# A new instruction order for a cross-attention kernel: fewer runs of small tiles on TensorE, fixed PSUM banks, four group slots

## The reference

```python
def layer0(x, c):
    q, k, v = heads(x @ Wq), heads(c @ Wk), heads(c @ Wv)        # 16 heads of 64
    logits = einsum('bhqd,bhkd->bhqk', q, k) / 8 + col_bias      # -20*(1-mask) on four columns
    out = einsum('bhqk,bhkd->bhqd', softmax(logits), v)
    return merge(out) @ Wo + bo + x

def layer(x, c):                                                 # layers 1, 2 and 3
    xn = x * rsqrt(mean(x * x) + 1e-5) * norm_w
    q, k, v = xn @ wq, c @ wk, c @ wv                            # 16 heads, 4 key-value heads, of 8
    attn = softmax(einsum('btgrd,bsgd->bgrts', q, k) / sqrt(8))
    return x + einsum('bgrts,bsgd->btgrd', attn, v) @ wo
```

## Time and profile before

| | |
|---|---|
| median of three runs | 1382.42 us (1378.57 to 1383.25) |
| span of the profiled execution | 1376.3 us |
| TensorE busy, matmuls | 1362.7 us, 99% of the span |
| TensorE busy, weight loads (overlap the matmuls) | 1055.6 us, 77% |
| VectorE, ScalarE, GpSimd busy | 1064.6, 1003.3 and 734.9 us: 77%, 73% and 53% |
| chain that ended last | TensorE 95%, ScalarE 2%, VectorE 2% |
| TensorE clock granted | 1.000 in all the span |

### The profile page before, as it was taken

The page is one execution under the profiler, slowest core; times in us unless marked ns, Lnnn a source line. Parts: engine busy times, 40 slices in busy tenths (PEclk is TensorE's granted clock), DMA queues, the critical chain, the costliest instruction groups (busy, mean ns, idle before and its releaser), DMA issues.

```text
span 1376.3 us, 59054 instructions
## 1 busy us (share of the span) xinstructions
PE 1362.7 (99%) x25494; PEld 1055.6 (77%) x25494; DVE 1064.6 (77%) x2258; ACT 1003.3 (73%) x2207; POOL 734.9 (53%) x851
## 2 busy tenths in 40 slices
PE   9999999999999999999999999999999999999997
PEld 7777777777777777777787777777777777777875
DVE  4487777987778977778777788777798777778776
ACT  4667777767778677777677786777776777767886
POOL 5355456654456545466554565544665445655553
PEclk9999999999999999999999999999999999999999
DMA  5010010000000010100001001001011010010000
GB/s 151 18 30 22 15 34 16 26 27 23 26 23 22 27 27 23 28 18 26 26 24 26 23 22 27 27 24 28 17 27 27 23 27 25 19 36 22 7 23 14
DMA packets 46003, 37.02 MB, mean 27 GB/s; under 512 B 17072, under 2 KB 41520, under 8 KB 45744
## 3 DMA queue, kind: packets, MB, share of 16 engines
q1 hardware_dynamic: 44576, 32.89, 8.8%
q10 hardware_dynamic: 1168, 0.36, 0.1%
HBM read 16.42 MB, written 4.19 MB: 15 GB/s over the span
## 4 chain that ended last, share of the span: by engine, by line
PE 95%; ACT 2%; DVE 2%; issue 0%; POOL 0%; DMA 0%; SPq 0%; POOLq 0%
PE psum L954 18%; PE psum L942 16%; PE psum L1009 10%; PE psum L1027 8%; PE psum L969 8%; PE psum L991 7%; PE psum L1055 7%; PE psum L1019 5%; PE psum L980 5%; PE psum L1063 4%; PE psum L1032 3%; PE psum L961 2%; PE psum L1038 2%; ACT E L1141 1%; ACT E L1136 1%; DVE st L1226 1%
## 5 line engine op out<-in xcount | busy, mean ns | idle before, releaser
L892 POOL TENSOR_TENSOR E<-E,st 128x512 f32<-128x512 f32 x488 | 497.3, 1044 | 168.1 <-DVE st L1238 159.4
L1136 ACT ACTIVATE E<-E,inv 128x512 f32<-128x512 f32 x384 | 273.4, 722 | 135.8 <-DVE E L1230 134.3
L1226 DVE TENSOR_REDUCE st<-psum 128x8 f32<-128x512 f32 x372 | 240.4, 673 | 145.5 <-PE psum L991 145.1
L1235 DVE TENSOR_REDUCE st<-E 128x8 f32<-128x512 f32 x488 | 321.2, 665 | 35.3 <-ACT E L1129 28.2
L1141 ACT COPY E<-psum 128x512 f32<-128x512 f32 x512 | 275.1, 609 | 33.7 <-PE psum L1009 33.5
L954 PE MATMUL psum<-wv,cT 128*128 128x374 f32 (+1 forms) x768 | 273.3, 486 | 0.3 <-issue 0.3
L1230 DVE TENSOR_TENSOR E<-psum,st 128x512 f32<-128x512 f32 x372 | 248.3, 677 | 0.3
L904 POOL TENSOR_TENSOR nt<-nt,powers 128x2 f32<-128x2 f32 (+1 forms) x102 | 19.9, 196 | 420.0 <-DVE nt L1265 400.2
L942 PE MATMUL psum<-cT,wk 128*128 128x256 f32 x1024 | 240.5, 383 | 0.2 <-DMA cT<-in_ctx_t 0.2
L942 PEld LDWEIGHTS psum<-cT,wk 128*128 128x128 f32 x1024 | 191.5, 190 | 34.8 <-issue 1.5
L954 PEld LDWEIGHTS psum<-wv,cT 128*128 128x128 f32 x768 | 138.2, 189 | 73.5 <-ACT V L1097 8.5
(11 more groups left out here) (68 smaller groups left out, 1632.2 us busy)
## 6 DMA issues: line engine op xcount, KB each, us to landing
KB<-K SPq DMA_DIRECT2D x1536, 8.0 KB
cT<-in_ctx_t SPq DMA_DIRECT2D x32, 256.0 KB, 2.8
xq<-in_x_t SPq DMA_DIRECT2D x32, 128.0 KB, 2.1
out<-xT SPq DMA_DIRECT2D x30, 128.0 KB, 1.8
wk<-in_L_xattn_Wk SPq DMA_DIRECT2D x3, 256.0 KB, 5.8
wv<-in_L_xattn_Wv SPq DMA_DIRECT2D x2, 374.0 KB, 8.6
wq<-in_L_xattn_Wq SPq DMA_DIRECT2D x1, 512.0 KB, 7.7
wo<-in_L_xattn_Wo SPq DMA_DIRECT2D x1, 512.0 KB, 4.4
```

Of the source, the lines that this page charges most:

```text
L892: e.tensor_tensor(E3, E3, wide(stat[s][u][:, 16:24]), ALU.mult).then_inc(g_nrm.sem, 1)
L1136: e.activation(E[s][u][:, :], E[s][u][:, :], ACT.Exp, scale=inv[s][:, u // 2:u // 2 + 1]).then_inc(a_exp.sem, 1)
L1226: e.tensor_reduce(stat[s][u][:, 0:8].rearrange("p (r h) -> p r h", r=2), scores_of[g, l, u], AX, ALU.max).then_inc(d_max.sem, 1)
L1235: e.tensor_reduce(stat[s][u][:, 8:16], heads(E[s][u][:, :]), AX, ALU.add).then_inc(d_sum.sem, 1)
```

## The change

The tables of all five engines are replaced, with ends for groups 0 to 6 and 26 to 31. TensorE's steps of one small-tile shape now stand next to each other more often. The number of slots `NS` goes from three to four, and steps of four different groups are in progress at once. The bank of each step comes from a table too (`PE_BANKS`, `BANK_ENDS`) in place of the rule. The transposes `t` of a layer become two steps of 16 records, one for each half, with their own waits and places. `x2` is done as 64-row transposes (two for each half, each into its own bank), in the same 64x128 tiles as `t`; ScalarE's square (L1157) reads the two banks in one instruction. A hook for aligning the program before chosen steps is there, but its list `FRESH` is empty, so nothing is emitted.

```diff
-NS = 3
+NS = 4
-PERIOD = 42.042923
+PERIOD = 41.111607
 PE_TIME = {
-    "pv": {1: (-307.00785,), 2: (-275.6979,), 3: (-251.97787,)},
+    "pv": {1: (87.69763,), 2: (127.91302,), 3: (168.09796,)},
...
+PE_BANKS = {
+    "k": {0: ("6", "7", "0", "6")},
...
+FRESH = set()
...
-        for kind, layers in {**table, **{k: {**table.get(k, {}), **v} for k, v in at_ends.get(g, {}).items()}}.items():
+        for kind, layers in at_ends.get(g, table).items():
...
             if kind == "t":
-                return [[("et", g, l, 2 * p + i)] for p in halves(g, u) for i in range(2)]
+                return [[("et", g, l, 2 * u + i)] for i in range(2)]
...
-            evictors = held_until(st)
-            if st[0] == "s" and l > 0:
-                at = min(([i, i + 1, j, j + 1] for i in range(5) for j in range(i + 2, 7)),
-                         key=lambda four: max(free[i] for i in four))
-            else:
-                at = sorted(sorted(range(8), key=lambda i: free[i])[:len(evictors)])
+            evictors, at = held_until(st), banks_of(*st)
...
-                if kind != "t":
-                    emptied(w, [ev for evs in before[st] for ev in evs])
+                emptied(w, [ev for evs in before[st] for ev in evs])
+                if (kind, l, u) in FRESH:
+                    e.addr_align(256, max_nops=0)
...
                 elif kind == "t":
                     w.wait_ge(l_ident, "ident")
-                    for n, p in enumerate(halves(g, u)):
-                        emptied(w, before[st][2 * n] + before[st][2 * n + 1])
-                        if late(g, l):
-                            w.wait_ge(a_exp, ("exp", g, l, 2 * p), ("exp", g, l, 2 * p + 1))
-                        else:
-                            w.wait_ge(g_nrm, ("nrm", g, l, 2 * p), ("nrm", g, l, 2 * p + 1))
...
+                    if late(g, l):
+                        w.wait_ge(a_exp, ("exp", g, l, 2 * u), ("exp", g, l, 2 * u + 1))
+                    else:
+                        w.wait_ge(g_nrm, ("nrm", g, l, 2 * u), ("nrm", g, l, 2 * u + 1))
...
                     for p in halves(g, u):
-                        m = e.transpose(bank[:, 128 * p:128 * p + 128], xT[s][:, 128 * p:128 * p + 128], ident[:, :])
+                        for i in range(2):
+                            rows = slice(64 * i, 64 * i + 64)
+                            m = e.transpose(psum[:, at[i], 64 * p:64 * p + 64], xT[s][rows, 128 * p:128 * p + 128],
+                                            ident[rows, rows])
...
-                        e.activation(QT[s][:, 2, tokens], bank[:, tokens], ACT.Square).then_inc(a_ev.sem, 1)
+                        e.activation(sq, x, ACT.Square).then_inc(a_ev.sem, 1)
```

More of the change, by code:

```diff
@@ L65 @@
[L65 to L72, removed]
+    "k": {0: (2.50397, 14.44440, 4.26196, -8.93698)},
@@ L73 @@
+    "pv0": {0: (62.41330, 60.00031)},
+    "x2": {1: (70.81265,), 2: (102.44397,), 3: (132.58655,)},
+    "q": {1: (68.69162,), 2: (100.48978,), 3: (132.33356,)},
+    "pv": {1: (88.79163,), 2: (129.00702,), 3: (169.71564,)},
 }
 DVE_TIME = {
[L75 to L79, removed]
@@ new lines @@
+        "add": {0: (46.52356, 47.11856, 45.33356, 45.92856)},
+        "max": {0: (48.30956, 48.90556, 47.71356, 49.50156),
+                1: (74.08823, 75.28223, 72.56824, 71.97223),
+                2: (100.83659, 100.24059, 102.95458, 99.64458),
+                3: (133.79279, 132.00078, 134.38878, 131.40479)},
+        "sum": {0: (51.26056, 52.28056, 50.25256, 53.92356),
+                1: (79.13390, 81.20190, 78.02890, 77.40690),
+                2: (106.74059, 104.87459, 107.44559, 105.49659),
+                3: (139.76611, 138.46512, 139.17010, 137.86911)},
@@ L438 @@
[L438 removed]
+        "add": {0: (16.35077, 16.35098, 16.94678, 16.94699)},
+        "max": {0: (16.35120, 17.54257, 17.54279, 16.94720),
+                1: (91.33392, 88.71793, 87.52393, 89.91193),
+                2: (123.90860, 125.10062, 126.89261, 124.50461),
+                3: (164.01495, 165.20895, 165.80496, 163.41895)},
+        "sum": {0: (17.54300, 18.95239, 18.24524, 18.24545),
+                1: (99.84906, 100.55408, 94.31793, 97.51599),
+                2: (146.05966, 134.51395, 138.09000, 133.91794),
+                3: (178.11694, 181.81830, 184.27823, 183.34134)},
@@ new lines @@
+    3: {
+        "cT": {0: (68.87723,)},
+        "kr": {1: (45.81723,), 2: (34.76723,), 3: (56.86724,)},
+        "lt": {0: (68.39724,)},
+        "st": {0: (191.65358,)},
+    },
+    4: {
+        "cT": {0: (68.39734,)},
+        "kr": {1: (45.81734,), 2: (34.76733,), 3: (56.86734,)},
+        "lt": {0: (67.91734,)},
+        "st": {0: (191.65364,)},
+    },
+    5: {
+        "cT": {0: (69.27876,)},
+        "kr": {1: (46.21875,), 2: (35.16874,), 3: (57.26875,)},
+        "lt": {0: (68.79875,)},
+        "st": {0: (193.35536,)},
+    },
@@ new lines @@
+    6: {
+        "cT": {0: (69.27879,)},
+        "kr": {1: (46.21879,), 2: (35.16880,), 3: (57.26878,)},
+        "lt": {0: (68.79877,)},
+        "st": {0: (193.35542,)},
+    },
+    26: {
+        "cT": {0: (70.01911,)},
+        "kr": {1: (28.90794,), 2: (28.90815,), 3: (62.15113,)},
+        "lt": {0: (111.13136,)},
+        "st": {0: (217.24680,)},
+    },
+    27: {
+        "cT": {0: (70.01954,)},
+        "kr": {1: (28.90772,), 2: (28.90793,), 3: (28.90815,)},
+        "lt": {0: (136.34449,)},
+        "st": {0: (213.56986,)},
@@ L759, in xattn_kernel @@
             for i, evs in zip(at, evictors):
-                held[i], free[i] = evs, max(DUE[ev] for ev in evs)
+                held[i] = evs
             if st[0] == "s" and l == 0:
```

1389 lines of the change are left out of this document (957 added, 432 removed), and 102 rows, old and new, of tables (BANK_ENDS, DVE_ENDS, PE_ENDS).

## The result

The changed kernel takes 1418.3 us (median, 1416.2 to 1421.3) against 1381.6 for the kernel before on the same chip: a ratio of 1.027, 95% interval 1.025 to 1.029. Forecast were 1389 us and a range to 1402: the sign is right, the size is not.

The account below looks back on a forecast made before the run. TensorE, busy 99% of the span, was taken as the bound. 1376.3 - 17 (own work) + 18 (stops) + 8 (start) - 2 (drain) = 1383.3 us of span; the median, 6.1 above the span, 1389 us, range 1373 to 1402.

Parts of the forecast that it names:

- Part 1: TensorE's own work shrinks by 17 us (8 to 18), from fewer small-tile visits and a cheaper `x2`.
- the price of `x2`: The new `x2` on TensorE takes 0.12 us instead of 0.21, saving 8.6 us over 96.
- a group without a stop takes 0.8 us less: A group in the middle without a stop takes 0.8 us less than before, from visits, runs and `x2`.
- Part 2: TensorE's stops called "issue", at instruction packet boundaries, rise by 18 us (-6 to 26) in the new order.
- The floor of 3.7 us for 300 instructions: On TensorE, about 300 instructions can't pass a packet boundary in under 3.4 to 3.9 us; 3.7 taken.
- the work that I set against the floor: On TensorE 300 instructions take 2.2 to 2.3 us in the triple `pv`, 2.9 to 3.3 around the scores.
- its two ends: Stops outside the middle: 22 us over 24 groups become 24 with the ends.
- rival (a): Instruction packets stay hidden and nothing new stops on TensorE: 1371 us, or 1365; chance 0.14.
- rival (c): Chains too tight, TensorE waits for ScalarE's late copies at three places a group: +20 us, 1409 us; chance 0.07.
- Part 3: The ends: waits at the start add 8 us (3 to 13), the drain gives -2 us (-5 to +5).
- rival (b): Floor nearer 3.1 than 3.7, only boundaries in the triple `pv` stop: +9 instead of +18, 1380 us; chance 0.17.
- (d): `x2` on TensorE keeps its old price: +9 us on the forecast, 1398 us; chance 0.05.

Follow-up runs that it names:

- the aligned kernel: Changed kernel with one alignment a group (groups 3 to 26), v(g,0,1) starting 48 instructions past a packet boundary, padding jumped: 1386.6 us, ratio 1.0043.
- experiment 7: The aligned kernel with the old `x2`, a full-tile transpose into one bank for each half: 1392.2 us, ratio 1.0078.
- Experiments 1 to 5: On the changed kernel: packet boundaries placed well (1386.6 us) or badly (1455.5), small matmuls appended, program moved 64 instructions (1411.4), a k step moved to shorten runs (1413.7).
- the misaligned one: Same alignment as the aligned kernel but at a bad place, v(g,0,1) starting 168 instructions past a packet boundary: 1455.5 us, ratio 1.055.
- the probe: Changed kernel with 1280 small matmuls appended, 320 each of 64, 96, 128 and 160 columns: 3.5 to 3.7 us a packet with 64 columns.
- Experiments 7 to 9: Mostly on the aligned kernel: old `x2` (1392.2 us); other banks in part (1391.6) or throughout (1380.9); q0 and v exchanged (1392.4; with those tables 1435.4, 1381.9).
- the one with all banks: The aligned kernel (alignment from group 1) with a searched bank for every step of the whole program: 1380.9 us, ratio 0.9994.

## Why the prediction was right and wrong

**Part 1 (own work, -17 us): right.** -16.4 by the table, which is the count at the prices of the kernel before and so confirms the count; the price of `x2` has a test of its own. The one of layer 3 takes 0.17 us, and the transposes `t(g,0,0)` behind it take 0.05 less than behind the old form (0.495 in the aligned kernel, 0.546 in experiment 7), so 0.12, as priced; the one of layer 2 takes 0.27, ahead of another small shape. The forecast that a group without a stop takes 0.8 us less failed. From one `wo0` step to the next, before and changed:

```profile
871.34 0.92 PE L1027 MATMUL psum<-QT,wo 128*128 128x256 f32 x3
...
913.18 1.13 PE L1027 MATMUL psum<-QT,wo 128*128 128x256 f32 x4
```

```profile
765.70 0.60 PE L1606 MATMUL psum<-QT,wo 128*128 128x256 f32 x2
...
807.12 1.25 PE L1606 MATMUL psum<-QT,wo 128*128 128x256 f32 x5
```

41.84 and 41.42 us: half of the saving is there, the other half is in the waits of the missing term below.

**Part 2 (stops, +18 us): the mechanism right, the term too small.** By the table the stops rose by 34.5 us, 28.0 in the middle and 6.5 at the ends, far past my 18 and its upper bound of 26; in all they are 41.8 us, where I had 24, at most 32. The places were right: in each five groups two stops in the triple `pv` and three around the scores. I had put the kernel before at nine stops and 6 us in the middle; the table has 4.3.

The floor of 3.7 us for 300 instructions was not the step that failed. From `wo0` of group 3 to that of group 25 the changed kernel takes 940.4 us and the aligned one, with next to no stops there, 915.5: 24.9 us of stops. Taking the aligned kernel's trace and holding back each crossing of a boundary of the changed one until 3.7 us after the instruction 300 before it gives 940.4 us too; 3.8 from 308 back gives 940.5, while 3.9 from 300 gives 945.5 and 4.0 from 308 gives 945.1, both too long.

Two steps failed. The first is the work that I set against the floor: I took 0.94 us for a `pv` in a run, which now takes 0.89, and up to 3.3 us for 300 instructions around the scores. With the measured times the same floor gives stops of 1.6 us where I had 1.4, and of 0.7 to 0.9 where I had 0.4 to 0.8, 5.7 us per five groups instead of 4.7, so 24.9 instead of 20.7 over these 22 groups. The second, and the larger, is the ends: I took the pattern of the middle for the whole program and allowed 2 us for its two ends. Groups 25 to 31, where the pattern ends, have a dozen stops with some 11 us, and the first 160 us have two with 1.8 us at the place of the boundary. Experiments 1 to 5 leave no other cause. The rule of the Trainium skill ("Runtime: NRT & Kernel Launch", "Instruction fetch mechanics") that a crossing is mostly hidden, rival (a), fails here: 32 us of stops in the middle of the changed kernel, and 71 in that of the misaligned one by the same comparison; it holds again from 128 columns on in the probe.

**The missing term: +12 us of waits in the middle.** The sum had none. I had put rival (c) at 0.07, against it that TensorE waits for ScalarE nowhere in the middle now, which says nothing about an order in which every step stands elsewhere. Rival (c) was right on the tightness, at about half of the price that I gave it (0.4 to 0.5 us a group, 0.9 forecast), and only in part on the places: of the steps that are late in every group `s(g,2,0)` waits for ScalarE's copy of `q`, as (c) has it, but `v(g,0,4)` and `k(g,0,3)` wait for a bank and `q(g,1,0)` for VectorE's add. Experiments 7 to 9 show what these waits are: with the old `x2` more than half goes, with free banks a third, and when one is removed other steps are late instead. The new order has several chains at their limit, so a shorter step on TensorE shows only in part. What makes up the two thirds that other banks leave was not taken apart.

**Part 3 (fill +8, drain -2): right on the fill, near on the drain.** Waits in the first 160 us rose by 7.3, and busy time fell to 150.5 us, inside 147 to 155. Waits in the drain rose by 1.0 us where I had 2 less. I did not try which chain holds the fill back.

**Sum.** -16.4 + 34.5 + 12.0 + 7.3 + 1.0 = 38.4, against a span longer by 38.1. The span came out at 1414.4 us where I had 1383.3: of these 31 us, 16.5 are the stops', 12 the waits' and 3 the drain's, and own work and fill differ from the forecast by under 1 us each. Of rival (b) and (d) nothing is left.

**What the order is worth.** From `wo0` of group 3 to that of group 25 the kernel before takes 924.6 us, the changed one 940.4, the aligned one 915.5 and the one with all banks 911.3. So with nearly all of its stops in the middle and a third of its waits there gone, the new order is 13 us faster in the middle, and gives 16 back at the ends. No version tried is faster than the kernel before.

## What to carry to other kernels

Count instructions as well as microseconds: where small matmuls stand in a row, look for the places where a 256-instruction packet would be used up in less than 3.5 to 4 us, and place the boundaries, or keep such runs short. Don't judge a new order's waits by the old order's trace: ask of each step how long before it its bank and its inputs come free, and expect that a saving on a full engine shows only up to the next tight chain. A table of banks belongs to one order; exchange two steps, and it has to be made again.

## What the runs showed of the hardware

- In the probe with 64 and 96 columns TensorE never crossed two packet boundaries (256 instructions) in under 3.47 us, whether their work took 1.8 or 2.7 us (3.47 four times, at most 4.02). In the middle of the changed kernel 3.7 us from 300 instructions back, or 3.8 from 308, gives the measured time to 0.1 us in 940.
- The stops stand at one place of the program modulo 256 instructions: 27 of 28 at 191 to 193, and all 22 at 125 to 127 with the program moved by 64.
- A jump over some 200 padded slots (24 jumps raise the instruction queue's packets from 202 to 220) cost nothing: the step ahead of it is the same to 1 ns at 24 of 24 places of one kernel and 22 of 24 of another.
- A wait that ends 55 ns ahead of its step still costs 0.16 us from step to step, without an entry in the waits.
